# Attention row maxima: one rounded copy, transposed tile by tile, in place of a high half and a low half

## What is computed

```python
scores = jnp.einsum('bhqd,bhkd->bhqk', Q, K) / jnp.sqrt(jnp.float32(dk))
scores = jnp.where(causal, scores, NEG)
m = jnp.max(scores, axis=-1, keepdims=True)
e = jnp.exp(scores - m)
attn = e / jnp.sum(e, axis=-1, keepdims=True)
```

## Time and profile before

| | us |
|---|---|
| median of 3 runs | 3343.2 (3333.41 to 3347.28) |
| span of the profiled execution | 3337.4 |
| TensorE busy in it | 2641.8 (79%) |
| ScalarE busy | 1912.7 (57%) |
| VectorE busy | 1763.9 (53%) |

### The profile page before, as it was taken

How to read it: one execution, slowest core, us unless ns; L and a number is a source line. 1 busy time by engine, 2 the same in 40 slices (tenths; PEclk the granted TensorE clock), 3 DMA queues, 4 the chain that set the end, 5 groups by cost and what they waited for, 6 DMA issues and landing times.

```text
span 3337.4 us, 46425 instructions
## 1 busy us (share of the span) xinstructions
PE 2641.8 (79%) x18736; PEld 1529.0 (46%) x18736; DVE 1763.9 (53%) x2698; ACT 1912.7 (57%) x1960; POOL 3.6 (0%) x12
## 2 busy tenths in 40 slices
PE   8999999777997789877898688986889868897215
PEld 4666456343563435534355344553445534453102
DVE  5463574545656355553555545654455544563524
ACT  2433435875358753586445864468534685447994
POOL 0000000000000000000000000000000000000000
PEclk7997989659896588966899668986779867987557
DMA  3000000000000000000000000000000000000000
GB/s 128 2 1 1 20 1 1 1 1 8 1 1 1 1 8 1 1 1 0 8 1 1 1 0 8 2 1 1 0 5 2 1 1 0 4 1 1 0 0 6
DMA packets 4561, 18.68 MB, mean 6 GB/s; under 512 B 608, under 2 KB 864, under 8 KB 3808
## 3 DMA queue, kind: packets, MB, share of 16 engines
q1 hardware_dynamic: 4320, 15.38, 1.2%
HBM read 13.28 MB, written 2.10 MB: 5 GB/s over the span
## 4 chain that ended last, share of the span: by engine, by line
PE 54%; ACT 19%; DVE 15%; issue 12%; DVEq 0%; DMA 0%; ACTq 0%; SPq 0%
ACT back_cosines L1320 6%; PE one_ps L1164 2%; PE two_ps L1275 2%; PE one_ps L862 2%; PE two_ps L910 2%; ACT back_cosines L1322 2%; PE one_ps L1710 2%; DVE back_nsum L1330 2%; PE one_ps L1717 2%; ACT L1320 2%; PE one_ps L766 1%; PE one_ps L1723 1%; DVE back_cosines L1393 1%; ACT L1862 1%; PE two_ps L862 1%
## 5 line engine op out<-in xcount | busy, mean ns | idle before, releaser
L1320 ACT ACTIVATE back_cosines<-back_cosines 128x2048 f32<-128x2048 f32 x256 | 472.2, 1899 | 0.5
L933 ACT ACTIVATE front_scratch<-one_ps 128x1152 f32<-128x1152 f32 x168 | 171.5, 1021 | 225.0 <-PE one_ps L848 224.8
L1322 ACT ACTIVATE back_cosines<-back_cosines,wts 128x2048 f32<-128x2048 f32 x128 | 252.4, 1994 | 41.1 <-DVE back_cosines L1393 40.9
L1330 DVE TENSOR_REDUCE back_nsum<-back_cosines 128x8 f32<-128x2048 f32 x64 | 144.4, 2281 | 234.0 <-ACT back_cosines L1320 234.0
L797 DVE TENSOR_REDUCE front_negm<-one_ps 128x8 f32<-128x1024 f32 (+1 forms) x168 | 204.4, 1220 | 56.6 <-PE one_ps L772 55.5
L837 PE MATMUL one_ps<-ident_bf,mask_q 128*128 128x256 bf16 x480 | 93.3, 302 | 80.5 <-ACT front_scratch L933 69.3
L696 ACT ACTIVATE back_cosines<-two_ps,wts 128x512 fp32r<-128x512 f32 x28 | 19.3, 688 | 224.1 <-PE two_ps L910 224.1
L766 PE MATMUL one_ps<-front_qkr 32*128 32x128 f32 (+1 forms) x896 | 136.5, 414 | 14.1 <-issue 8.9
L1393 DVE TENSOR_SCALAR back_cosines<-two_ps 128x2048 f32<-128x2048 f32 x56 | 128.2, 2290 | 28.5 <-PE two_ps L1257 28.3
L933 ACT ACTIVATE back_cosines<-two_ps 128x1152 f32<-128x1152 f32 (+1 forms) x84 | 86.0, 1024 | 92.0 <-PE two_ps L848 92.0
L766 PEld LDWEIGHTS one_ps<-front_qkr 32*128 32x128 f32 x896 | 96.6, 274 | 88.5 <-DVE front_negm L797 46.3
(11 more groups left out here) (630 smaller groups left out, 5795.1 us busy)
## 6 DMA issues: line engine op xcount, KB each, us to landing
wts<-w_dram SPq DMA_DIRECT2D x1, 4184.0 KB, 15.3
front_xin<-x_dram SPq DMA_DIRECT2D x8, 256.0 KB, 4.2
out_dram<-back_z SPq DMA_DIRECT2D x8, 256.0 KB, 2.1
wts<-w_dram SPq DMA_DIRECT2D x1, 1736.5 KB, 19.1
wts<-w_dram SPq DMA_DIRECT2D x1, 1199.0 KB, 5.3
wts<-w_dram SPq DMA_DIRECT2D x1, 1152.0 KB, 16.5
wts<-w_dram SPq DMA_DIRECT2D x3, 256.0 KB, 5.8
wts<-w_dram SPq DMA_DIRECT2D x1, 516.5 KB, 4.8
```

What stands on the lines that cost most here:

```text
L933: nc.scalar.activation(h.probs[:, e % 2, 0:n * HEADW].rearrange("p (k c) -> p k c", c=HEADW), h.ps[:, 0:n, 0:HEADW], ACT.Exp, scale=float( ...
L1320: nc.scalar.activation(cosines, cosines, func, scale=scale).then_inc(h.arc_pass.sem, 1)
L1322: nc.scalar.activation(cosines, cosines, func, scale=scale, bias=C(bias)).then_inc(h.arc_pass.sem, 1)
L1330: nc.vector.tensor_reduce(h.nsum[:, kt, :].rearrange("p (g2 j) -> p j g2", g2=2), h.cosines[:, u % 2, kt * 4 * TOK:(kt + 1) * 4 * TOK].rea ...
```

## The change

`negm` is now of the rounded type (fp32r), so the reduction itself rounds the maximum as it writes it. The second column of a group stays zero. The four transposes in fp32 against the fp32 identity become four ordinary matmuls in fp32r against a rounded identity `ident_r`, which VectorE casts once at the start. The first three wait only for the last reduction but one; there is one more `yield`; the fourth waits for the last reduction and writes a second PSUM bank. VectorE then copies 384 columns and, one `yield` later, 128 columns of the result into `maxTr`. The copies into the second column, the high half and the low half are gone, and so are the signals `max_pair` and `negm_high` and two columns of constants. The tables of runs have entries that are one larger on TensorE, where a step came in, and smaller by one on VectorE, where one went.

```diff
-            self.negm, self.maxTr = sb("negm", [P, TILES, P]), sb("maxTr", [P, TOK], F32R)
+            self.negm, self.maxTr = sb("negm", [P, TILES, P], F32R), sb("maxTr", [P, TOK], F32R)
...
-            yield
-            pe.wait_ge(h.max_pair.sem, h.max_pair.at(turn, s))
+            yield from max_end_pe(pe, h, turn, s, MSETS)
+
+        def max_end_pe(pe, h, turn, s, sets):
+            yield
+            pe.wait_ge(h.max_done.sem, h.max_done.at(turn, s, sets - 1))
             for t in range(TILES):
-                last = nc.tensor.transpose(h.ps[:, 0, t * P:(t + 1) * P], h.negm[:, t, :], C("ident"))
-            last.then_inc(h.negm_ps.sem, 1)
+                if t == TILES - 1:
+                    yield
+                    pe.wait_ge(h.max_done.sem, h.max_done.at(turn, s, sets))
+                last = nc.tensor.matmul(h.ps[:, t // (TILES - 1), t % (TILES - 1) * P:(t % (TILES - 1) + 1) * P],
+                                        h.negm[:, t, :], ident_r[:], start=True, stop=True, skip_group_check=True)
+                if t >= TILES - 2:
+                    last.then_inc(h.negm_ps.sem, 1)
...
-        def max_end_dve(dve, h, turn, s, sets):
-            yield
-            dve.wait_ge(h.max_done.sem, h.max_done.at(turn, s, sets))
-            for t in range(TILES):
-                last = nc.vector.tensor_copy(max_columns(h, slice(t, t + 1), 1)[:, 0], max_columns(h, slice(t, t + 1), 0)[:, 0])
-            last.then_inc(h.max_pair.sem, 1)
-            yield
-            dve.wait_ge(h.negm_ps.sem, h.negm_ps.at(turn, s))
-            high_dve(dve, h.ps[:, 0, :], h.high[:, 0, :], "m_sign", h.negm_high)
-            yield
-            dve.wait_ge(h.negm_high.sem, h.negm_high.at(turn, s))
-            split_dve(dve, h.ps[:, 0, :], h.high[:, 0, :], "m_low", h.maxTr[:, :], h.negm_ready)
+        def max_end_dve(dve, h, turn, s):
+            for i, columns in enumerate((slice(0, (TILES - 1) * P), slice((TILES - 1) * P, TOK))):
+                yield
+                dve.wait_ge(h.negm_ps.sem, h.negm_ps.at(turn, s, i + 1))
+                nc.vector.tensor_copy(h.maxTr[:, columns], h.ps[:, i, 0:columns.stop - columns.start]).then_inc(h.negm_ready.sem, 1)
...
+            nc.vector.tensor_copy(ident_r[:], C("ident")).then_inc(consts_ready, 1)
```

More of the change, by code:

```diff
@@ L354, in __init__ @@
             parts = scratch[:, 8 * TOK:12 * TOK]
-            self.negm = scratch[:, 12 * TOK:13 * TOK].rearrange("p (t c) -> p t c", t=TILES)
+            self.negm = rounded("negm", [P, TILES, P], 12 * TOK)
             self.y = sb("y", [P, TOK])
@@ L410, in __init__ @@
         self.negm_clear = signal("negm_clear", {"causal2": 1})
-        self.max_pair = signal("max_pair", {s: 1 for s in CAUSAL + ("mqa",)})
-        self.negm_high = signal("negm_high", {s: 1 for s in CAUSAL + ("mqa",)})
-        self.negm_ps = signal("negm_ps", {s: 1 for s in CAUSAL + ("mqa",)})
-        self.negm_ready = signal("negm_ready", {s: 1 for s in CAUSAL + ("mqa",)})
+        self.negm_ps = signal("negm_ps", {s: 2 for s in CAUSAL + ("mqa",)})
+        self.negm_ready = signal("negm_ready", {s: 2 for s in CAUSAL + ("mqa",)})
         self.score_ps = signal("score_ps", {s: CSETS for s in CAUSAL} | {"linear": CSETS, "mqa": QSETS, "arccos": 2 * UNITS})
@@ L1128, in mqa_pe @@
                         last.then_inc(h.max_ps.sem, 1)
-            yield
-            pe.wait_ge(h.max_pair.sem, h.max_pair.at(turn, s))
-            for t in range(TILES):
-                last = nc.tensor.transpose(h.ps[:, 0, t * P:(t + 1) * P], h.negm[:, t, :], C("ident"))
-            last.then_inc(h.negm_ps.sem, 1)
+            yield from max_end_pe(pe, h, turn, s, 2 * TILES)
             for e in range(QSETS + 1):
```

31 lines of the change are left out of this document (15 added, 16 removed), and 34 rows, old and new, of tables (DVE_RUNS, PE_RUNS).

## The result

The changed kernel takes 3373.0 us in the median of 19 executions (3339.2 to 3392.1), the kernel before 3335.5 us beside it (3324.5 to 3354.6): a ratio of 1.0078, with a 95% interval of 1.0057 to 1.0098 (the two medians alone would give 1.011). It is slower by about 0.8%. I had said 3346 us, and 3332 to 3359.

A forecast was written before the change was run, and what follows sets the result against it. No engine bounds throughout; TensorE makes 54% of the chain, and ScalarE covers most handover waits. Loop, prologue and set-up terms summed to +2.6 us on the 3343.2 us median, 3345.8, stated as 3346 us; range 3332 to 3359 us.

The forecast's parts named there:

- place 1: Loop, transposes after the linear attention's L910: waiting 384-column copy delays the next product 0.3 us, +1.8 us over six rounds.
- place 2: Loop, transposes that start without a wait: 384-column copy delays the front half's reductions, +0.3 us, +1.8 us over six rounds.
- The waits of the earlier trace: TensorE's waits for pair copies and new scores, 40.9 us, 1.2% of the span; to fall under 10 us.
- place 3: Loop, TensorE waits 1.63 us for the maxima; ScalarE takes the scores 5.6 us after they end: 0 us gain.
- end (c) of the prologue: Second half of causal1: reductions now start after the copy, so L862, already waiting 0.87 us, moves later: +1.1 us.
- the prologue's other ends: Five ends in the prologue, put at -1.0, +0.3, -0.7, -0.9 and 0 us.
- Step (f) of the sum: First half of causal1 in the prologue and two epilogue ends: each 0 us, with 0.6 us on either side.
- the clock 0.05: Rival: ordinary matmuls keep the clock at its upper level, gaining under 10 us, 3337 us; chance 0.05.
- place 3 and 4: Two loop places holding twelve of 32 ends; scores wait for ScalarE by 5.6 and 1.0 us: 0 us.
- The rival of the copy of 384 columns that blocks: Copy waits for TensorE and holds other-half work behind it; 20 ends outside arccos cost 22 us, 3365 us; chance 0.12.

The follow-up runs named there:

- the old order: Changed kernel with VectorE's epilogue table as before at one place, so a residual addition again precedes the other half's high half: 3378.5 us, ratio 1.0105 to the kernel before.
- before_matmul: Kernel before with rounded maxima and ordinary fp32r matmuls in place of the four transposes, all else kept: 3349.8 us, ratio 1.0030 to the kernel before.
- late_transpose: Changed kernel with both copies in VectorE's second slot, behind the other half's work, and fp32 transposes put back: 3324.7 us, ratio 0.9960 to the kernel before.
- late_matmul_place1: As late_transpose, but with ordinary fp32r matmuls at place 1 and two ends of the prologue: 3346.6 us, ratio 1.0027 to the kernel before.
- transpose_mode: Changed kernel with its four matmuls put back to fp32 transposes; rounded maxima, waits and the two copies stay: 3347.6 us, ratio 1.0035 to the kernel before.
- late copies: Changed kernel with both copies in VectorE's second slot, behind the other half's work (early: as changed); with matmuls 3363.3 us, ratio 1.0069 to the kernel before.
- fp32_matmul: Changed kernel with its four operations as ordinary fp32 matmuls, neither fp32r nor transpose mode: 3362.3 us, ratio 1.0066 to the kernel before.
- matmul_twice: Changed kernel with each of the four fp32r matmuls made twice at place 1 and two ends of the prologue: 3383.5 us, ratio 1.0137 to the kernel before.
- before_delay: Kernel before with a small extra VectorE reduction behind the pair copies, 0.5 us at place 1, 0.25 us at place 2: 3330.2 us, ratio 0.9964.

## Why the prediction was wrong

**What held.** Places 1 and 2 lose by the order of VectorE's queue, 0.49 and 0.26 us from the transposes to the next product, where I said 0.3 and 0.3. The waits of the earlier trace rows are gone, nothing is won by it at place 3, where ScalarE takes the first scores 7.9 us after they end (2671.92 + 0.42), and end (c) of the prologue waits 2.07 us.

```profile
2671.92 0.42 PE L843 MATMUL one_ps<-front_maxTr,max_rows 32*128 32x128 f32 x3
...
2680.23 1.11 ACT L928 ACTIVATE front_scratch<-one_ps 128x1152 f32<-128x1152 f32 x1
```

VectorE's busy time fell by less than the 40 to 48 us I gave, for two reasons: the copies take 0.56 us for 384 columns and 0.28 us for 128, where I had 0.5 and 0.2, and the four pair copies that went had held VectorE for 0.41 us together, not for four times 0.168 us. At place 1 the third matmul ends 0.90 us after the first starts, the upper end of my 0.6 to 0.9 us. Of the prologue's other ends I can't say what each gave: the whole prologue takes 393 to 417 us in the profiles, and 395.5, 403.9 and 403.5 us in the three of the changed kernel alone.

**Step (f) of the sum failed.** It said "the two ends in the epilogue: I put each at 0", with 0.6 us on either side. The epilogue costs 5.3 us more in all three profiles of the changed kernel (483.7 us), and 0.5 us more with the old order. I had read the tables' entries as "smaller by one"; in the epilogue 3, 5, 3 had not become 2, 5, 3 but 2, 3, 1, 2, 2, which carried an operation past a wait.

**The sum took the clock for fixed, and that failed.** I gave the clock 0.05 and only as a gain, where "ordinary matmuls in place of transposes kept it at the upper level". At place 1 they do the opposite: with fp32r matmuls the first L996 took 2.07 us in all 40 rounds (two to six) of eight kernels. What place 1 costs shows when the start of the same ScalarE instruction is taken in one round of each kernel (the third; the fifth of before_matmul, the fourth of before), less the round's start, less the same for late_transpose (us):

| kernel | at 60 us, first exponential after place 1 | at 98 us, behind place 2 | at 279 us | end of round |
|---|---|---|---|---|
| late_matmul_place1 | 1.3 | 1.3 | 2.8 | 3.4 |
| transpose_mode | 0.5 | 1.4 | 3.0 | 3.4 |
| before_matmul | 1.3 | 2.0 | 3.1 | 3.4 |
| changed | 3.3 | 4.3 | 3.9 | 3.9 |
| before | 0.0 | 0.7 | 1.4 | 3.0 |

Early copies cost 0.5 us at place 1 with transposes, the fp32r matmuls 1.3 us with late copies, and both together 3.3 us. L996 runs wholly at the low clock in both kernels with matmuls, but in these rounds the rise comes at 62.8 us with early copies and at 59.0 us with late ones. Place 2 adds 0.9 to 1.0 us with early copies. My +0.3 and +0.3 us for these places measured a gap; at place 2 the changed kernel is 3.6 us behind the kernel before. Behind it, in the stretches of place 3 and 4, the kernels draw together, and one that is 1.3 us late there ends as late as the others. The last column is the round's length less 406.2 us. The kernel before ends 3.0 us late as well, so of the 3.9 us only 0.9 us are the change's: over a whole round most of what place 1 and place 2 cost is made up again. That is also why the parts do not add: from late_transpose any one of them costs about 3 us in each round, and the second hardly more.

The clock alone doesn't set that price. The second rounds of late_transpose and of transpose_mode, which both rise early:

```profile
817.80:1224.10 406.30, 331.11 (x2340) 191.60 (x2340) 214.84 (x319) 240.26 (x246) 0.00 (x0) 0.80 0.01 2
```

```profile
810.00:1219.50 409.50, 329.96 (x2340) 190.87 (x2340) 214.99 (x320) 240.26 (x246) 0.00 (x0) 0.81 0.01 2
```

The second is 3.2 us longer at a clock that is no lower: TensorE idles 79.5 us in it and 75.2 us in the first. So 1.4 us of delay at places 1 and 2 brought further waits later in the round.

The rival of the copy of 384 columns that blocks (0.12, 3365 us) came nearest in its time and had the right place: early copies cost 23 us with transposes (3347.6 against 3324.7), where I had 22 us. That the numbers agree is luck. I had them as 20 waits of 1.1 us; what is found at place 1 is a wait that is 0.5 us longer, and the larger part of the 23 us comes later, partly from further waits as above. What each of them costs is not shown.

In the median, transposes give the changed kernel 8 us (3355.7 to 3347.6, within the intervals) and with late copies 38 us (3363.3 to 3324.7, well clear of them). Late copies give nothing with matmuls, where the lower clock takes back what they gain, and 23 us with transposes. The prediction's range was left because the clock's cost, 0.002 to 0.006 of mean clock or 6 to 17 us by the slope above, came on top of some 10 us of waits and epilogue: 4.5 us at places 1 and 2 in six rounds, 5.3 us in the epilogue, and 10 us by the comparison at equal clock.

**What stays open.** Why the clock rises earlier behind fp32 than behind fp32r, at equal length of the four operations (1.12 us), no run tells. Nor why rounds come out at 406.2, 409.5 or 412 to 413 us and seldom between; why one kernel's median lay at 3373 us once and at 3356 us twice; and why the epilogue took 506.5 to 507.8 us in the profiles of late_matmul_place1, fp32_matmul and matmul_twice, at a granted clock of 0.69 (0.73 in the changed kernel's). The last matters most. The epilogue of late_matmul_place1 holds the same instructions as that of late_transpose (487.1 us), and matmul_twice's the same as the changed kernel's (483.7 us). First late_transpose, then late_matmul_place1:

```profile
2846.30:3333.40 487.10, 273.99 (x1944) 142.00 (x1944) 230.22 (x277) 327.88 (x285) 0.00 (x0) 0.72 0.01 2
```

```profile
2853.70:3360.20 506.50, 292.67 (x1944) 151.14 (x1944) 230.42 (x278) 327.96 (x285) 0.00 (x0) 0.69 0.01 2
```

So the clock's course can make 19 to 24 us of difference in one stretch without a single other instruction in it, as much as the whole loss. The longer executions of the changed kernel, 3364 to 3392 us, were not profiled. Where they lose their time, and whether it is there, is not known.

## What to carry to other kernels

When a table of numbers sets the order, compare the rows that it produces over the whole program, the short last stage too: one pair that changes places can cost more than all that was removed. An early copy that waits for TensorE is not free for the other half behind it; put it behind the work that is ready. Where a kernel changes between the two levels of the clock, the length of a small delay is not its price: 1.4 us of it came out as 3 us a round in transpose_mode, and an added operation made before_delay quicker. Such a change is judged by many timed executions on either side, also compared at an equal mean clock, and not by the sum of gaps or by one profile.

## What was not expected of the hardware

Behind fp32 transposes or fp32 matmuls at place 1 the clock was up 55.2 to 56.1 us into the round in 51 of the 55 rounds (two to six) of eleven profiled kernels. The other four lie at 58.5 to 65.3 us. Behind fp32r matmuls it was up at 58.9 to 64.9 us in all 40 rounds of eight. The first round of the loop, which follows the prologue, is left out: there either kind has early and late rises, from 54.2 to 64.6 us, so what TensorE did before place 1 counts as well. The Trainium skill, "TensorE: Matmul & The Clock Gate", Part 4, says that transposes in transpose mode don't count as work for the clock. Here the kernels with transposes have the earlier rise and mostly the higher mean clock (0.795 to 0.803, against 0.787 to 0.795 with fp32r matmuls at place 1), and the measurement decides. No run shows a stretch with transposes alone. An fp32r matmul of 128x128 takes as long as an fp32 transpose, 0.66 us for four at the upper level and 1.12 us at the lower; an ordinary fp32 one is two instructions and takes longer.
